# Cross attention with scores formed already turned and values in 32-column tiles, inside a gated block on one core

## What is computed

```
scores = einsum('bgnqd,bgkd->bgnqk', qg, k) * scale
scores = where(causal, scores, -1e30)
attn   = softmax(scores)
out    = einsum('bgnqk,bgkd->bgnqd', attn, v)
x      = x + tanh(g_xattn) * (out @ w_out.T)
```

## Time and profile before

| what | us |
|---|---|
| median of 3 runs | 525.49 |
| lowest, highest | 520.78, 527.2 |
| the profiled execution, its own time | 523.37 |
| its span in the profile | 521.5 |
| PE busy in the span | 462.1 |
| DVE, ACT, POOL busy | 376.3, 269.7, 234.3 |

### The profile page before, as it was taken

The page is one execution under the profiler, slowest core; times in us unless marked ns, Lnnn a source line. Parts: engine busy times, 40 slices in busy tenths (PEclk is TensorE's granted clock), DMA queues, the critical chain, the costliest instruction groups (busy, mean ns, idle before and its releaser), DMA issues.

```text
span 521.5 us, 10743 instructions
## 1 busy us (share of the span) xinstructions
PE 462.1 (89%) x3316; PEld 418.4 (80%) x3316; DVE 376.3 (72%) x1179; ACT 269.7 (52%) x725; POOL 234.3 (45%) x318
## 2 busy tenths in 40 slices
PE   0159999989976799999999999999999998589996
PEld 0149999978855589999999999999999997578895
DVE  4876578785655787877878787788887778944544
ACT  2048877767511255565655645555556557263342
POOL 7944424921024644544544645446355431161251
PEclk9999999999998999999999999999999999997899
DMA  8100000020002434334243243352442320000011
GB/s 288 17 3 2 1 1 2 5 79 1 3 20 62 96 67 121 83 80 134 57 136 77 60 141 80 80 141 60 101 120 60 80 62 1 1 1 1 1 41 41
DMA packets 19882, 31.42 MB, mean 60 GB/s; under 512 B 6020, under 2 KB 8200, under 8 KB 19848
## 3 DMA queue, kind: packets, MB, share of 16 engines
q1 hardware_dynamic: 15928, 22.31, 17.5%
q10 hardware_dynamic: 3920, 8.69, 5.5%
HBM read 13.16 MB, written 1.05 MB: 27 GB/s over the span
## 4 chain that ended last, share of the span: by engine, by line
PE 76%; DVE 14%; ACT 4%; issue 4%; DMA 2%; POOL 0%; SPq 0%; DVEq 0%; ACTq 0%; POOLq 0%
PE bank L1195 40%; PE bank L1148 6%; PE bank L1275 5%; PE bank L1238 5%; PE bank L1266 4%; PE bank L1131 3%; PE bank L1276 2%; PE bank L1237 2%; ACT PR L515 2%; PE bank L1100 1%; PE bank L1122 1%; PE bank L1079 1%; DMA cst_sb<-in_cst 1%; DVE small L656 1%; PE bank L1354 1%
## 5 line engine op out<-in xcount | busy, mean ns | idle before, releaser
L411 POOL TENSOR_TENSOR room<-room,qk_room 128x512 f32<-128x512 f32 x64 | 82.4, 1288 | 104.6 <-DMA qk_room<-qk_room 104.6
L555 ACT ACTIVATE PR<-sm,nm 128x128 f32<-128x128 f32 (+1 forms) x128 | 57.2, 448 | 117.3 <-DVE nm L927 117.3
L1195 PE MATMUL bank<-hH,qk_parts 128*128 128x512 f32 x256 | 81.2, 399 | 0.0
L850 DVE SCALAR_TENSOR_TENSOR qk_room<-bank,qk_bias,cst_sb 128x512 f32<-128x512 f32 x64 | 48.0, 750 | 37.5 <-PE bank L1195 33.6
L1195 PE MATMUL bank<-hL,qk_parts 128*128 128x512 f32 x128 | 62.0, 485 | 9.2 <-DVE room L850 6.1
L1195 PEld LDWEIGHTS bank<-hH,qk_parts 128*128 128x128 f32 x256 | 48.7, 190 | 9.9
L515 ACT ACTIVATE PR<-bank,nxm 128x128 f32<-128x128 f32 (+1 forms) x128 | 45.8, 435 | 14.7 <-DVE nxm L820 12.4
L1148 PE MATMUL bank<-PTs,room 128*128 128x128 f32 x384 | 50.7, 276 | 0.1
L850 DVE SCALAR_TENSOR_TENSOR room<-bank,qk_bias,cst_sb 128x512 f32<-128x512 f32 x64 | 47.5, 743 | 0.0
L1148 PEld LDWEIGHTS bank<-PTs,room 128*128 128x128 f32 x384 | 46.6, 192 | 0.3 <-ACT PTs L231 0.3
L1195 PE MATMUL bank<-woH,o_parts 128*128 128x256 f32 x256 | 46.5, 280 | 0.0
(11 more groups left out here) (198 smaller groups left out, 1271.2 us busy)
## 6 DMA issues: line engine op xcount, KB each, us to landing
qk_room<-qk_room SPq DMA_DIRECT2D x128, 128.0 KB, 2.3
stg<-in_wqkv ACTq DMA_DIRECT2D x6, 768.0 KB, 4.6
stge<-in_we ACTq DMA_DIRECT2D x7, 256.0 KB, 3.4
stg<-in_wqkv SPq DMA_DIRECT2D x2, 768.0 KB, 6.4
stgo<-in_wo ACTq DMA_DIRECT2D x6, 256.0 KB, 3.8
x_sb<-in_x SPq DMA_DIRECT2D x4, 256.0 KB, 6.3
out_y<-yacc SPq DMA_DIRECT2D x4, 256.0 KB, 2.1
cst_sb<-in_cst SPq DMA_DIRECT2D x1, 520.0 KB, 7.1
```

Source lines behind the costliest of these rows:

```text
L411: pool.tensor_tensor(v, v, qk_sw[:, q, :], ALU.subtract).then_inc(s["rope_done"], 1)
L555: ins = act.activation(PR[:, q, a:e], sm[:, q, a:e], ACT.Exp, bias=nm[:, q, t:t + 1], scale=-1.0, accum_out=rs[:, q, t:t + 1])
L850: return dve.scalar_tensor_tensor(out.rearrange("p (b t) -> p b t", b=2), O_B[q][:, :].rearrange("p (b t) -> p b t", b=2), qk_bias[:, c:c ...
L1195: ins = pe.matmul(outp, l, r, start=(m == 0), stop=(m == n - 1))
```

## The change

- The first scores stay, but serve for the maxima only. DVE writes the negated maxima as bf16, eight for each group of three pieces (`nxm` [P, 3, 8]), and `x_scores(p)` waits for the maximum of piece p - 2 (`s_max`) where it waited for its exp.
- `x_turned` replaces `x_turn`: the scores are formed a second time, with the keys stationary and the queries of four heads moving (512 columns, bf16), so that they come out as [key, query]. In two of three blocks a matmul of 512 columns adds the turned mask. Then four matmuls of 128 columns add the negated maxima: the stationary operand is one column of `nxm` repeated over 128 columns, the moving one the identity. The blocks of a group are (key half, query half) = (0,0), (0,1), (1,1), from `block_of`.
- exp is one ACT instruction per block, 128 by 512, from PSUM without bias, into one of four buffers `probs`. `pt_copy`, its 48 copies and its semaphores go.
- `x_values` has a stationary operand of 32 columns (VP = 32) and writes head n to partitions 32n to 32n + 31 of bank 4, one matmul per head.
- The lags grow: `x_turned` is TLAG = 3 pieces behind `x_scores`, `x_values` VLAG = 5. The work set into the loops moves with them, `residual` by four pieces into the next batch, and the last `norm_turn` goes behind the loop.
- POOL's memset clears 1024 columns of `room` where it cleared 4192.

```diff
-VP, VZ = 128, 96
+VP = 32
+TLAG, VLAG = 3, 5
...
-        room = sb("room", [P, VZ + 4 * NT * P])
+        room = sb("room", [P, 4 * NT * P])
...
-        PR = sb("PR", [P, 2, 512])
-        PTs = sb("PTs", [P, 2, 512])
+        probs = sb("probs", [P, 4, 512])
+        PR = probs[:, 0:2, :]
+        PTs = probs[:, 2:4, :]
...
-        v_slots = room[:, VZ:VZ + NT * XG * VP].rearrange("p (n d) -> p n d", d=VP)
+        v_slots = room[:, 0:NT * XG * VP].rearrange("p (n d) -> p n d", d=VP)
...
-        nxm = sb("nxm", [P, 2, 4])
+        nxm = sb("nxm", [P, 3, 8], BF16)
...
             return (g, 0, [4 * g + n for n in range(4)]) if j == 0 else (g, 1, [4 * g + 2 * (j - 1) + n for n in range(2)])
+
+        def block_of(z):
+
+            return ((0, 0), (0, 1), (1, 1))[z]
 
...
         m7 = {e: n for n, e in enumerate(M7)}
         NPX = XP * B
-
-        def copied_by_act(p):
-            return p % 3 != 0
-
-        def copier(p):
-
-            by_act = [copied_by_act(n) for n in range(p + 1)]
-            return ("pt_copy_act", sum(by_act)) if by_act[p] else ("pt_copy_dve", p + 1 - sum(by_act))
 
         def steps(eng, step, peeled=1):
 
...
 
 
-            link(pool.memset(room[:, :], 0.0))
+            link(pool.memset(room[:, 0:NT * XG * VP], 0.0))
             pool.memset(v_slots[:, :, XD:XD + 1], 1.0).then_inc(s["va_ready"], 1)
 
             pool.wait_ge(s["d_rows"], 16)
@@ -482,6 +472,8 @@
             def q_evac(b, X, t):
                 n = m6["Q", b, X, t]
                 act.wait_ge(s["m6_pe"], n + 1)
+                if b:
+                    act.wait_ge(s["st_pe"], XP * (b - 1) + 6 * (X + 1))
                 act.activation(qT[:, X, t, :, :].rearrange("p h n -> p (h n)"), bank_bf[0][:, :], ACT.Copy).then_inc(s["m6_free"], 1)
 
             def o_evac(b):
@@ -500,35 +492,30 @@
                     act.wait_ge(s["o_pe"], m - 1)
                 act.activation(oT[:, m % 2, :], bank[4][:, 0:256], ACT.Copy).then_inc(s["oT_ready"], 1)
 
+            def x_exp(p):
+
+                act.wait_ge(s["st_pe"], p + 1)
+                if p >= 4:
+                    act.wait_ge(s["pv_pe"], p - 3)
+                act.activation(probs[:, p % 4, :], PT_B[p % 2][:, :], ACT.Exp).then_inc(s["s_exp"], 1)
+
             q_evac(0, 0, 0)
             q_evac(0, 0, 1)
-            for p in range(NPX):
+            for p in range(NPX + VLAG):
                 b, k = divmod(p, XP)
-                g, t, heads = piece(k)
-                width = P * (t + 1)
-                if p >= 2 and copied_by_act(p - 2):
-                    pt_copy(act, p - 2)
-                act.wait_ge(s["s_max"], p + 1)
-                if p >= 2:
-                    act.wait_ge(s["pt_pe"], p - 1)
-                for n, h in enumerate(heads):
-                    ins = act.activation(PR[:, p % 2, n * width:(n + 1) * width], S_B[p % 2][:, n * width:(n + 1) * width],
-                                         ACT.Exp, bias=nxm[:, p % 2, n:n + 1])
-                ins.then_inc(s["s_exp"], 1)
-                if k in (2, 3):
-                    q_evac(b, 1, k - 2)
-                if k == 5 and b:
-                    o_evac(b - 1)
-                if k in (7, 9) and b + 1 < B:
-                    q_evac(b + 1, 0, (k - 7) // 2)
-                if k == 4 and b >= 2:
+                if p < NPX:
+                    if k in (3, 4):
+                        q_evac(b, 1, k - 3)
+                    if k == 8 and b:
+                        o_evac(b - 1)
+                    if k in (9, 10) and b + 1 < B:
+                        q_evac(b + 1, 0, k - 9)
+                if TLAG <= p < NPX + TLAG:
+                    x_exp(p - TLAG)
+                if k == 7 and b >= 2:
                     h_high(b - 2)
-                if p >= 5 and p % 3 == 2:
-                    oT_evac((p - 5) // 3)
-            for p in range(NPX - 2, NPX):
-                if copied_by_act(p):
-                    pt_copy(act, p)
-            oT_evac(NPX // 3 - 1)
+                if p >= 7 and p % 3 == 1:
+                    oT_evac((p - 7) // 3)
             h_high(B - 2)
             o_evac(B - 1)
 
@@ -811,36 +798,39 @@
                 dve.wait_ge(s["m7_free"], m7["NT", b] + 1)
                 dve.memset(small[:, 110:111], 0.0).then_inc(s["hT_ready"], 1)
 
-            for p in range(NPX):
+            def x_max(p):
+
                 b, k = divmod(p, XP)
                 g, t, heads = piece(k)
+                m, z = divmod(p, 3)
+                a = (0, 4, 6)[z]
                 dve.wait_ge(s["s_pe"], p + 1)
-                if p >= 2:
-                    dve.wait_ge(s["s_exp"], p - 1)
-                dve.tensor_reduce(nxm[:, p % 2, 0:len(heads)], S_B[p % 2][:, :].rearrange("p (h n) -> p h n", h=len(heads)),
+                if z == 0 and m >= 3:
+                    dve.wait_ge(s["st_pe"], 3 * (m - 2))
+                dve.tensor_reduce(nxm[:, m % 3, a:a + len(heads)], S_B[p % 2][:, :].rearrange("p (h n) -> p h n", h=len(heads)),
                                   AX.X, ALU.max, negate=True).then_inc(s["s_max"], 1)
-                if p >= 2 and not copied_by_act(p - 2):
-                    pt_copy(dve, p - 2)
+
+            for p in range(NPX + VLAG):
+                b, k = divmod(p, XP)
+                if p < NPX:
+                    x_max(p)
                 if p == 0:
                     rsqrt_step(SM(124, 6), SM(56, 6), SM(130, 6), 6)
                 if p == 1:
                     pack(0, 1)
                 if k == 1 and b + 1 < B:
                     norm_q(b + 1)
-                if k == 2 and b >= 2:
+                if k == 6 and b >= 2:
                     hidden_t(b - 2)
-                if p >= 6 and p % 3 == 0:
-                    norm_out((p - 6) // 3)
-                if k == 5 and b + 1 < B:
+                if p >= 9 and p % 3 == 0:
+                    norm_out((p - 9) // 3)
+                if k == 6 and b + 1 < B:
                     pack(b + 1, 0)
-                if k >= 6 and b:
-                    residual(b - 1, k - 6)
-                if k == 10 and b + 1 < B:
+                if k == 11 and b + 1 < B:
                     pack(b + 1, 1)
-            for p in range(NPX - 2, NPX):
-                if not copied_by_act(p):
-                    pt_copy(dve, p)
-            norm_out(NPX // 3 - 2)
+                b1, phase = divmod(p - XP - 10, XP)
+                if b1 >= 0 and phase < 6:
+                    residual(b1, phase)
             hidden_t(B - 2)
             norm_out(NPX // 3 - 1)
 
@@ -1117,36 +1107,43 @@
                 if k == 0:
                     pe.wait_ge(s["m7_free"], b + 1)
                 if p >= 2:
-                    pe.wait_ge(s["s_exp"], p - 1)
+                    pe.wait_ge(s["s_max"], p - 1)
                 for n, h in enumerate(heads):
                     pe.matmul(S_B[p % 2][:, n * width:(n + 1) * width], qT[:, h // 8, t, h % 8, :], kT[:, b, g, 0:width], start=True, stop=False)
                     ins = pe.matmul(S_B[p % 2][:, (n + 1) * width - P:(n + 1) * width], ident_bf, mask_bf, start=False, stop=True)
                 ins.then_inc(s["s_pe"], 1)
 
-            def x_turn(p):
+            def x_turned(p):
+
+                b, k = divmod(p, XP)
+                m, z = divmod(p, 3)
+                g, h = k // 3, 4 * (k // 3)
+                kt, t = block_of(z)
+                pe.wait_ge(s["s_max"], 3 * m + (1 if z == 0 else 3))
+                if p >= 2:
+                    pe.wait_ge(s["s_exp"], p - 1)
+                by_head = PT_B[p % 2][:, :].rearrange("p (h n) -> p h n", h=4)
+                pe.matmul(by_head, kT[:, b, g, kt * P:(kt + 1) * P], qT[:, h // 8, t, h % 8:h % 8 + 4, :], start=True, stop=False)
+                if kt == t:
+                    pe.matmul(by_head, mask_bf, ident_bf.unsqueeze(1).to_broadcast([P, 4, P]), start=False, stop=False)
+                for n in range(4):
+                    ins = pe.matmul(PT_B[p % 2][:, n * P:(n + 1) * P], nxm[:, m % 3, 4 * t + n:4 * t + n + 1].to_broadcast([P, P]), ident_bf,
+                                    start=False, stop=(n == 3))
+                ins.then_inc(s["st_pe"], 1)
+
+            def x_values(p):
+
+                b, k = divmod(p, XP)
+                m, z = divmod(p, 3)
+                kt, t = block_of(z)
                 pe.wait_ge(s["s_exp"], p + 1)
-                if p >= 2:
-                    pe.wait_ge(s[copier(p - 2)[0]], copier(p - 2)[1])
-                for n in range(4):
-                    ins = pe.transpose(PT_B[p % 2][:, n * P:(n + 1) * P], PR[:, p % 2, n * P:(n + 1) * P], ident)
-                ins.then_inc(s["pt_pe"], 1)
-
-            def x_values(p):
-
-                b, k = divmod(p, XP)
-                g, t, heads = piece(k)
-                m = p // 3
-                pe.wait_ge(s[copier(p)[0]], copier(p)[1])
                 if p == 0:
                     pe.wait_ge(s["va_ready"], 1 + B)
-                if t == 0 and m:
+                if z == 0 and m:
```

(63 more changed lines are left out.)

1 line of the change is left out of this document (removed).

## The result

The changed kernel takes 508.07 us (median of 4 runs, 506.74 to 508.53), the kernel before 525.62 (also of 4); the ratio of the runs is 0.9675, with a 95% interval of 0.962 to 0.9731. Some executions of a kernel are slower as a whole by over 1.5%, and all ratios here leave those out. The forecast was 512.6, so the gain of 17.6 us was larger than the 13 expected.

The account below looks back on a forecast made before the run. PE's stream bounds the stage: -43.2 - 21.1 + 28.4 + 28.8 - 4.5 = -11.6 us, giving 511.8 from the profiled execution or 513.9 from the median; forecast 512.6, range 499 to 535.

Parts of the forecast that it names:

- PE sets the pace: Cross-attention stage: PE busy 98.6 of 104 us at full clock, so an edit counts by its effect on PE's stream.
- Removed and added streams: PE's stream in the stage: old values 43.2 and transposes 21.1 us removed, x_turned's matmuls 28.4 us added.
- The values, 28.8: x_values on 32-column tiles: 48 pieces at 0.56 us plus 0.04 for tile changes, 28.8 us of PE.
- Only the second half of head n and the first of head n + 1 can overlap: x_values on PE: two halves of one head follow each other, making five slots instead of eight, 0.56 us a piece.
- rival 1: x_values: all four strips side by side, 0.22 + 0.04 us a piece, 499.5 us for the kernel; chance 0.15.
- So nearly nothing; I allow 0.04 a piece: PE around x_values: changing from 128 by 128 to 128 by 32 tiles and back costs 0.04 us a piece.
- rival 3: x_values: overlap as forecast, but the array drains at both tile changes, 0.56 + 0.32 us a piece, 526 us; chance 0.12.
- Idle, net 4.5 off: PE's waits in the stage: 5.5 us of idle gone, 1.0 added at the end; bounds 0 and 7 off.
- The last norm_turn, 1.0: End of the stage: norm_turn of the third batch, ahead of the first projection, waits for residual on DVE, 1.0 us.
- DVE at nothing: DVE in the stage: loses 11.0 us of copies, some 68 of about 100 us busy, beneath PE, so no cost.
- the 3 us that I named as a sign of being wrong: PE's waits in the stage: forecast wrong if DVE's maxima appear among them with more than 3 us.
- Two of the signs: Profile after: x_values' eight instructions start within some 0.6 us; first projection of the self attention starts near 131 us.

Follow-up runs that it names:

- two experiments: Changed kernel with the values of a group's three blocks issued back to back (503.65 us); changed kernel without the mask matmul of x_turned (502.52 us).
- the grouped kernel: Changed kernel with the values of a group's three blocks issued back to back in one step: 503.65 us, ratio 0.9611 to the kernel before.
- the last one: Changed kernel with three blocks' values back to back, last norm_turn behind first projection, others one piece later, three batches' pack copies on ACT: 495.64 us.

## Why the prediction was right, point by point

- **PE sets the pace.** Held: 13.8 us less of stream, by measured prices, gave a stage 15.8 shorter. At the end it held only in part: of 7.8 and 7.0 us taken out in two experiments 4.3 and 4.4 arrived, in the second some 6 without the slow clock.
- **Removed and added streams.** 43.2 and 21.1 removed, 28.4 added by x_turned: the starts 61.24, 61.45 and 61.67 confirm 0.22 for 512 columns and for the four maxima, and the repeated column cost nothing.
- **The values, 28.8.** This term was mis-sized: 48 x 0.46 = 22.1. Both of its parts were wrong, in opposite directions. "Only the second half of head n and the first of head n + 1 can overlap" failed, and with it "starts are in order": the first four instructions start within 0.03 us, which on one strip lie 0.11 apart, so halves of different strips all overlap (0.22, rival 1). "So nearly nothing; I allow 0.04 a piece" for the change of tile failed: 0.24 (rival 3 had 0.32). The rule of the Trainium skill that I weighed there, in TensorEngine Tiling (Array Packing), section Tiling Modes, that a change of the tiling mode drains the array, fits the gaps of the values; the grouped kernel agrees, with one pair of gaps for three pieces. The earlier trace rows stay as they were read: there the change cost nothing that the starts show, and why, no run shows. What the Trainium skill says in TensorE: Matmul & The Clock Gate, section Packing small matmuls, that matmuls on different column tiles run side by side, holds here for fp32 pairs too: four strips took 0.22 of stream where one took 0.85 (0.99 less 0.14). That the total came near is in part luck: per piece 0.34 too much for the halves and 0.20 too little for the changes, 16.3 and 9.6 us in 48 pieces; only the difference, 6.7, shows in the sum.
- **Idle, net 4.5 off.** The stage gives 15.8 - 13.8 = 2.0. The waits for ACT went as said, and with PE the bound the idle does vanish: the turned kernel on wide tiles absorbed over 6 us (7.3 more work, 0.9 longer). On the faster stream 3.4 came back at norm_turn and 2.1 at the maxima.
- **The last norm_turn, 1.0.** It cost 2.00 us.
- **DVE at nothing.** Wrong in kind: 69.0 of 95.8 us is room enough on average, but its copies and residual's steps stretch beside POOL's work, and the maxima wait behind them, in the changed kernel for 2.1 us. That is under the 3 us that I named as a sign of being wrong. Moving the copies took 2.6 us of PE's waits off.
- **The rest.** 1.3 us at the start and 2.0 behind the stage had no term; both lie in code or a transfer that the change leaves alone, and show in one execution only. Two of the signs failed with the values: the starts spread over 0.15 and not 0.6, and the first projection starts at 125.4, not near 131.

Taking the measured terms: -43.2 - 21.1 + 28.4 + 22.1 - 2.0 = -15.8, against -11.6 forecast. The difference is 6.7 from the values less 2.5 from idle; all of PE's recorded waits in the stage are for DVE. That the two halves of the change alone give far less than the whole was in no rival; I had priced the whole, and the waits of ACT only as an idle term.

Not settled: no run moved residual's steps out from before the maxima, so what the last wait of 2.5 us is worth stays open. Nor does any run part the longer lags from the turned scores: the kernel with turned scores alone has both.

## What to carry to other kernels

In this kernel fp32 matmuls with outputs of 32 rows on different partition strips of one bank ran side by side, so the longest strip set the price and not their number; but going to the narrow tile and back cost about 0.24 us, so collect such matmuls before switching. Before pricing an edit to one engine, check who waits second: two edits that gain 1.1% and 0.5% alone, because each frees the engine that the other one loads, gained 3.3% together. And read the granted clock before comparing two stages: in three of these runs it fell behind a wait of PE and hid part of a gain. A DVE instruction's price in a quiet place is not its price beside POOL's work.

## What was not expected of the hardware

- Eight fp32 value instructions on four strips start within 0.15 us, the first four of them within 0.03; eight on one strip over 0.78.
- Changing the tile from 128 by 128 to 128 by 32 left 0.10 us empty, changing back 0.12 to 0.14, whatever number of matmuls (8 or 24) stood between.
- A 256-column bf16 copy on DVE, 0.21 us alone, lasted up to 1.31 us, to the end of the POOL operation beside it (to within 0.1); the same copy on ACT took 0.42.
- The granted clock fell to its 1.2 GHz level inside the stage behind waits of PE of 2.2 and 2.83 us, and stayed at 1.00 in the grouped kernel behind waits of 2.15 and 2.40 and in the last one behind 2.55.
